# A new order of work in a fused attention and feed-forward kernel: later projection, moved weight sums, and a weight ring filled in three transfers a step

## The reference

```
xn  = layernorm(x)
att = layernorm(linear_attention(xn; 16 heads, elu+1) @ W_proj.T + b_proj) * gamma + beta + xn
h   = silu(xn @ w1.T * s1) * (xn @ w2.T * s2)          # 256 -> 1024
h   = gelu(h @ h1.T * sh1);  h = gelu(h @ h2.T * sh2)   # 1024 -> 1024, twice
out = x + att + (h @ w3.T) * s3                         # 1024 -> 256
```

## Time and profile before

| what | value |
|---|---|
| median of 3 runs | 1734.03 us (1733.47 to 1736.09) |
| profiled execution, whole | 1730.4 us |
| its span, first to last instruction | 1728.5 us |
| PE / PEld busy | 1562.2 us (90%) / 1438.9 us (83%) |
| DVE / ACT / POOL busy | 1213.1 us (70%) / 969.2 us (56%) / 501.1 us (29%) |
| moved by DMA | 298.15 MB |

### The profile page before, as it was taken

One profiled execution on the slowest core, in us unless ns is written; L12 is line 12 of the kernel. 1 busy time (PEld: TensorE's weight loads), 2 busy tenths in 40 slices (PEclk: granted clock), 3 DMA queues, 4 the chain that ended last, 5 costly groups with the idle time before them and its releaser, 6 DMA issues.

```text
span 1728.5 us, 32973 instructions
## 1 busy us (share of the span) xinstructions
PE 1562.2 (90%) x10956; PEld 1438.9 (83%) x10956; DVE 1213.1 (70%) x2083; ACT 969.2 (56%) x1745; POOL 501.1 (29%) x573
## 2 busy tenths in 40 slices
PE   6474999999999999999999999999999999999997
PEld 4474888888988888898888989888898888889897
DVE  3574686876868677685867768686685867768585
ACT  3243465655647465565755656565564656556463
POOL 3221150422314133240512314052231413323040
PEclk8697999999999999999999999999999999999999
DMA  6885255371735536173462626437172553717343
GB/s 229 316 325 187 92 205 182 109 255 51 263 106 182 195 112 234 57 252 138 140 232 91 228 89 227 162 116 254 52 260 98 195 186 113 243 43 261 129 159 132
DMA packets 84962, 298.15 MB, mean 172 GB/s; under 512 B 7232, under 2 KB 44224, under 8 KB 59584
## 3 DMA queue, kind: packets, MB, share of 16 engines
q0 software_dynamic: 37152, 238.04, 39.3%
q1 hardware_dynamic: 47344, 58.49, 10.0%
q10 hardware_dynamic: 432, 1.18, 0.2%
HBM read 280.91 MB, written 23.07 MB: 176 GB/s over the span
## 4 chain that ended last, share of the span: by engine, by line
PE 43%; DVE 20%; issue 16%; ACT 10%; DMA 4%; POOL 3%; DVEq 1%; SPq 0%; ACTq 0%; POOLq 0%
PE ps L830 19%; PE ps L859 7%; PE ps L804 5%; DVE partial_sums L1284 4%; PE ps L709 4%; DVE operands_a L1261 4%; PE ps L710 3%; PE ps L711 3%; DVE values_a L1253 3%; DVE operands_b L1261 2%; ACT operands_a L1008 2%; ACT values_out L1033 2%; ACT gate_ring L971 2%; POOL values_a L609 2%; DMA weight_set<-in_w_ffn 2%
## 5 line engine op out<-in xcount | busy, mean ns | idle before, releaser
L830 PE MATMUL ps<-operands_a,hidden_weights 128*128 128x256 f32 x5376 | 755.1, 286 | 61.6 <-DVE operands_a L1261 36.7
L830 PEld LDWEIGHTS ps<-operands_a,hidden_weights 128*128 128x128 f32 x5376 | 686.4, 191 | 88.1 <-DVE operands_a L1261 49.4
L830 PE MATMUL ps<-operands_b,hidden_weights 128*128 128x256 f32 x1792 | 298.2, 288 | 56.9 <-DVE partial_sums L1284 42.1
L830 PEld LDWEIGHTS ps<-operands_b,hidden_weights 128*128 128x128 f32 x1792 | 247.3, 191 | 69.6 <-DVE partial_sums L1284 45.8
L1284 DVE TENSOR_TENSOR partial_sums<-partial_sums,ps 128x512 f32<-128x512 f32 x320 | 214.3, 681 | 126.1 <-PE ps L830 125.5
L1261 DVE TENSOR_TENSOR operands_a<-values_a,operands_a 128x512 fp32r<-128x512 f32 x336 | 272.2, 825 | 41.9 <-ACT operands_a L996 22.3
L625 POOL DMA_DIRECT2D hidden_weights<-weight_blocks x252 | 138.0, 548 | 523.4 <-PE ps L830 510.6
L804 PE MATMUL ps<-xnT,w_ffn 128*128 128x512 f32 x1024 | 252.2, 401 | 15.3 <-DVE values_a L1253 15.3
L804 PEld LDWEIGHTS ps<-xnT,w_ffn 128*128 128x128 f32 x1024 | 191.7, 190 | 59.9 <-DVE values_a L1253 16.2
L1033 ACT ACTIVATE values_out<-partial_sums,vectors 128x256 f32<-128x256 f32 x192 | 86.9, 500 | 181.1 <-DVE partial_sums L1284 179.6
L1008 ACT ACTIVATE operands_a<-values_a 128x512 fp32r<-128x512 f32 x192 | 120.9, 630 | 107.8 <-POOL values_a L619 49.3
(11 more groups left out here) (112 smaller groups left out, 2083.2 us busy)
## 6 DMA issues: line engine op xcount, KB each, us to landing
hidden_weights<-weight_blocks POOLq DMA_DIRECT2D x192, 1024.0 KB, 5.6
hidden_weights<-weight_blocks POOLq DMA_DIRECT2D x64, 512.0 KB, 3.8
raw_weights<-weight_blocks SPq DMA_DIRECT2D x48, 272.0 KB, 5.5
x<-in_H SPq DMA_DIRECT2D x16, 512.0 KB, 5.1
weight_set<-in_w_ffn SPq DMA_DIRECT2D x16, 512.0 KB, 10.7
out_dram<-acc SPq DMA_DIRECT2D x32, 256.0 KB, 2.2
weight_blocks<-in_w_ffn SPq DMA_DIRECT2D x12, 512.0 KB, 10.6
weight_blocks<-weight_set SPq DMA_DIRECT2D x4, 1536.0 KB, 7.2
```

Of the source, the lines that this page charges most:

```text
L830: r = mm(bank[:, m * HT:(m + 1) * HT], ring_weights[:, place, 2 * g + j, m * P:(m + 1) * P], as_used(buf[:, j, slot[block_of_b], part, :]) ...
```

## The change: what it does

1. **Matmul order in a product.** The loop over the two halves m of the output goes inside the loops over group and part. All four matmuls of one group's hi (or lo) follow each other, so that the second group's hi is first needed at half the product and its lo at three quarters, where it was a quarter and three eighths.
2. **Ring parts.** Three transfers a step: block 1; blocks 5, 6, 7; blocks 2, 4, 3 (512, 1536, 1536 KB), each begun when the last product that uses it is through.
3. **Banks.** Even steps use banks 4, 5, 0 and odd ones 1, 2, 3; step 0's first product waits for the sixth gate group's value in place of the seventh's.
4. **Order on PE.** `kv_sums(1)` goes behind gate group 5, gate group 2 ahead of `apply_kv`; both `proj_step`s go from before step 1 to behind its second product. In tile 0 the transposes for tile 1 go from step 2 to step 3.
5. **Order on DVE, ACT and POOL.** `ln2_apply` (three passes over 128x1024) goes from the middle of step 3 to the end of the tile, behind the last `lo_of_output`; the last `output` goes behind all of the k, v work. `keep_first`, `add_u` and the second sum get waits for the GELU of the step before, which reads the same scratch. `keep_first(0)` is ahead of four conversions; `k_act_step` waits for `q_made`.
6. **Weight sets.** POOL's `weight_sums` is gone: DVE makes the sums of set 0 in the prologue, of set 1 in step 0, of set 2 in step 1 and of set 3 in step 2. SP loads set 2 after set 1 is stored and set 3 after step 1's last product; x of tile 1 is requested ahead of the store of set 3. SP no longer waits for `proj_weights` first, and DVE no longer for the warm-up.

Of the diff, the parts that the steps rest on:

```diff
-RING_PARTS = ((0, 1), (1, 2), (3, 2), (5, 2))
-PART_OF = {1: 0, 5: 1, 6: 1, 7: 2, 2: 2, 4: 3, 3: 3}
+RING_PARTS = ((0, 1), (1, 3), (4, 3))
+PART_OF = {1: 0, 5: 1, 6: 1, 7: 1, 2: 2, 4: 2, 3: 2}
-BANKS = ((0, 1, 4), (5, 2, 3), (0, 1, 4), (5, 2, 3))
-PART_FREE = ((1, 6, 2, 3), (1, 5, 7, 4), (1, 6, 7, 3), (1, 5, 7, 4))
+BANKS = ((4, 5, 0), (1, 2, 3), (4, 5, 0), (1, 2, 3))
+PART_FREE = ((1, 7, 3), (1, 7, 4), (1, 7, 3), (1, 7, 4))
...
-        return {(0, 1): gated(6), (0, 6): gated(6), (0, 5): gated(5),
+        return {(0, 1): gated(5), (0, 6): gated(5), (0, 5): gated(6),
...
@@ SP, tile 0
                         store_sums(1)
                         sp.wait_ge(s_stored[1], 32)
+                        load_set(2)
+                        copy_blocks(2)
+                        store_sums(2)
+                        sp.wait_ge(*prod.after(t, "1P4"))
                         load_set(3)
                         copy_blocks(3)
+                        load_x(t + 1, first)
                         store_sums(3)
-                        sp.wait_ge(s_stored[3], 32)
-                        load_x(t + 1, first)
@@ SP, prologue
-                sp.wait_ge(s_proj_raw, 16)
                 load_set(0)
                 copy_blocks(0)
-                sp.wait_ge(s_wproj, 2)
-                load_set(2)
                 store_sums(0)
-                copy_blocks(1)
-                store_sums(2)
                 sp.wait_ge(s_stored[0], 32)
                 load_set(1)
-                copy_blocks(2)
+                copy_blocks(1)
@@ PE, product
-                    for m in range(2):
-                        for g, group in enumerate(groups):
-                            buf, slot = operands(group)
-                            for part in range(2):
+                    for g, group in enumerate(groups):
+                        buf, slot = operands(group)
+                        for part in range(2):
...
+                            for m in range(2):
                                 for j in range(2):
@@ PE, body
                     product(t, 0, 3)
+
+                    product(t, 1, 1)
+                    product(t, 1, 6)
                     proj_step(t, 0)
                     proj_step(t, 1)
-
-                    product(t, 1, 1)
-                    product(t, 1, 6)
@@ ACT
             def keep_first(t, s):
                 act.wait_ge(*prod.after(t, f"{s}P1"))
+                if s > 0:
+                    act.wait_ge(*gelu.after(t, f"{s - 1}C21" if s % 2 else f"{s - 1}C12"))
@@ DVE
             def add_u(t, s):
                 dve.wait_ge(first_kept.sem, first_kept.at(t, s))
+                if s > 0:
+                    dve.wait_ge(*gelu.after(t, f"{s - 1}C12" if s % 2 else f"{s - 1}C21"))
                 sum_into(t, s, 6, 1, 0)
@@ DVE, prologue
-                    if checking:
-                        dve.wait_ge(s_warm, WARM_UP)
...
+                        sum_of_weights(0, 1)
+                        sum_of_weights(0, 3)
```

More of the change, by code:

```diff
@@ L680, in body @@
                             refill(t, 3, 2)
-                            refill(t, 3, 3)
                 return body
@@ L880, in body @@
                 def body(t, more):
+                    staging = isinstance(t, int) and t == 0
                     gate_group(t, 0)
@@ L920, in body @@
                     product(t, 2, 7)
-                    if more:
+                    if more and not staging:
                         transposes(t + 1, 0)
@@ L928, in body @@
                     product(t, 3, 6)
+                    if staging:
+                        transposes(t + 1, 0)
+                        transposes(t + 1, 1)
                     product(t, 3, 2)
@@ L1505, in body @@
                         check_piece(t, 0)
+                    if checking:
                         check_piece(t, 1)
-                        check_piece(t, 2)
-                    if checking:
-                        check_piece(t, 3)
-                    add_u(t, 3)
-                    lo_of_output(t, 0, "C12")
-                    add_v(t, 3)
+                    if more:
+                        transposed_lo(t + 1, 1)
+                    add_v(t, 3)
+                    lo_of_output(t, 0, "C22")
@@ new lines, in body @@
+                    add_c22(t, 3)
+                    lo_of_output(t, 0, "C21")
+                    lo_of_output(t, 0, "C12")
+                    add_c12(t, 3)
+                    add_c21(t, 3)
+                    lo_of_output(t, 1, "C22")
+                    lo_of_output(t, 1, "C12")
+                    if checking:
+                        check_piece(t, 2)
+                    if more:
+                        put_ones(t + 1)
+                    lo_of_output(t, 0, "C11")
+                    lo_of_output(t, 1, "C21")
@@ L1537, in body @@
-                    output(t, 1)
-                    if more:
                         z_step(t + 1, 2)
                         z_step(t + 1, 3)
+                        phi_k(t + 1, 0)
+                        if checking:
+                            check_piece(t, 3)
+                        phi_k(t + 1, 1)
                         phi_k(t + 1, 2)
                         phi_k(t + 1, 3)
+                    else:
+                        if checking:
+                            check_piece(t, 3)
+                            dve.wait_ge(piece_checked.sem, piece_checked.at(t, CHECKS - 1))
+                            v.tensor_reduce(low_max[:], low[:], AX_X, ALU.max).then_inc(s_low_step, 1)
+                        output(t, 0)
+                        if checking:
+                            dve.wait_ge(s_flag_sum, 1)
+                            v.tensor_copy(flag[:], att_bank(A_T0)[0:1, 0:1]).then_inc(s_flag, 1)
@@ L1544, in run @@
+                    output(t, 1)
                 over_tiles(dve, first, prologue, body)
```

299 lines of the change are left out of this document (145 added, 154 removed).

## The result

The changed kernel takes 1791.58 us (median of 4 runs, 1785.17 to 1793.6), the kernel before 1733.75 us beside it (1732.32 to 1736.09): ratio 1.0326, 95% interval 1.0297 to 1.0354. I had said 1646 us, and 1603 to 1692 as the range. The profiled execution of the changed kernel has this head, where the one before has 1728.5.

A forecast was written before the change was run, and what follows sets the result against it. PE was taken as the bound, its waits as what could be won. Tile 1 beginning at 169, 14 loop tiles of 97.9 and a last tile of 101.7 gave 1641.3 us span, predicted as 1646 us, range 1603 to 1692.

The forecast's parts named there:

- The stops for operands and sums: Product stretch of a loop tile: 8.5 us of PE stops go, one operand wait of 0.6 us stays.
- a floor of 93.6 us without the ring: Loop tile: 102.14 less 0.6 in the gate phase and 8.5 in products, plus 0.6 for one wait.
- `ln2_apply` at its later place: End of the loop tile: its move there costs PE 0, with 1 us of cover.
- The ring in three transfers: Loop tile: larger refills land after the products that need them, costing 4.3 us a tile.
- the 2.8 us for blocks 2, 4, 3 of step 3: Free after step 2's last product, needed two products or 3.8 us later, so late 2.8 us.
- The landing of 6.5 us: Time for 1536 KB to land in the ring, 6.6 us with POOL's wake of 0.1; bounds 5.1 and 9.6.
- Tile 0: First tile: tile 1 begins near 169 us in place of 197.2, 28 us earlier; bounds 42 and 10.
- The end: Last tile: more work ahead of the reduction adds 5.2 us; the last tile takes 101.7 us.
- The sum: Whole kernel: 169 + 14 x 97.9 + 101.7 = 1641.3 us span, 1643 profiled execution, 1646 predicted.
- The rivals: Alternative outcomes for the whole kernel: 1613 us (chance 0.17), 1684 (0.16), 1709 (0.06), 1871 (0.05), 1734 (0.02).
- The slower one: Loop tile: 1536 KB refills land in 12 us or more, 15 us a tile, 1871 us; chance 0.05.
- my three signs of being wrong: 1536 KB landings over 8 us, DVE releasing PE for over 2 us a tile, or tile 1 beginning after 187.

The follow-up runs named there:

- e1_four: Changed kernel with the ring filled in four smaller transfers a step in place of three: 1598.20 us, ratio 0.9198 to 0.9229.
- e5_small_x: Changed kernel with the load of the next tile's x cut from 512 KB to 64 KB: 1758.18 us, ratio 1.0126 to 1.0184.
- e8: Changed kernel with four ring transfers a step, plus raw weight block copies of sets 2 and 3 begun one set earlier: 1588.71 us.
- e6_block_waits: Changed kernel with the same three releases a step, but each block moved and waited for alone: 1669.47 us, ratio 0.9618 to 0.9653.
- e9: Changed kernel with added matmuls, results unused, before all six waits for the ring from tile 1 on: 1759.45 us, ratio 1.0134 to 1.0173.

## Why the prediction was wrong, point by point

- **The stops for operands and sums: right.** I took 8.5 us of stops off the products, left 0.6, and had a floor of 93.6 us without the ring. e1_four measures 93.44, and the one stop left in the tile read is 0.38 us, for an operand. `ln2_apply` at its later place costs PE nothing: no stop stands in the end of e1_four's tile.
- **The ring in three transfers: the step that failed.** The term was 4.3 us a tile; it measures 12.8. The mechanism was the one named, a part that lands behind the product that needs it; the size was off by three. By pair of steps I had 0.3, 1.2 and 2.8 us of stops; the trace has 3.08 (step 0 to 1), 3.40 (1 to 2) and 3.25 (2 to 3). So the 2.8 us for blocks 2, 4, 3 of step 3 was right (2.86), and the four stops of steps 1 and 2 measure 6.5 us where I had 1.5. Three things were missing. The landing of 6.5 us holds only for a transfer that runs alone: the chain has 9.19 us (issued at 757.63, behind the part beside which x is loaded) and 8.53 (777.24, behind the part issued at 773.47). POOL's issue begins 0.5 to 0.6 us after the product ends at the three refills of the chain, not 0.1, for which no row stood. And the clock, for which I had nothing, takes 2.2. Stops and clock make 11.9 of the 12.8 us; the last 0.9 I can't assign, and idle times are modelled.
- **What I read past.** The earlier trace rows had 9.6 us for two blocks amid traffic. I wrote it down as the upper bound of the landing and never worked out the stops that it gives. The estimate from the Trainium skill (DMA: Bandwidth & Descriptors, on the fixed cost of a transfer), 5.6 us for 1536 KB, would have made the error larger: the 1536 KB loads into the ring have medians from 6.5 us (e5_small_x) up.
- **Tile 0: 28 us forecast, 9 found, below my lower bound of 10.** The first gate and product came 5 us late (33.88 and 52.49 for 29 and 47.6), step 1 ended at 107.86 instead of 96, and blocks 5, 6, 7 of set 3 landed at 152.58 instead of 133. I had priced loads, sums and stores, and not the copies of raw blocks nor the wait of POOL for them. e8 shows 11 us of it, on the order with four transfers. Part of the other 8 stands in the chain, and I had it at nothing: I counted tile 0's products at full clock, and the granted clock from 52.49 to 188.15 is 0.82. Sixteen matmuls in the chain take there what thirty-two take at full clock:

```profile
82.84 3.76 PE ps L828 x16
...
90.46 3.80 PE ps L828 x32
...
104.05 3.79 PE ps L828 x16
...
152.72 3.75 PE ps L828 x16
```

  That is 1.9 us more at each of the three, 5.6 in all. No run takes it away, so how much earlier tile 1 would begin is not shown.
- **The end.** The last tile measures 1790.1 - 1675.59 = 114.5 against 101.7; without the ring's waits it is 102.7 (e1_four), so that term was right. (My 101.3 for the last tile before rested on one tile of 102.14; with the mean of 102.34 it is 98.6, and the forecast did not use it.)
- **The sum.** 14 x (106.25 - 97.9) = 117, tile 0 19, last tile 13: 149 us, all of the gap between 1643 and the profiled 1791.9.
- **The rivals.** The slower one was to decide from 10.3 us of ring waits a tile. That point was right, and the ring's 12.8 us passed it, with the clock; the stops alone, 9.7, fall just short of it. Its condition, a landing of 12 us or more, did not come: 9.19 is the longest in the chain of the loop tile. Its price (15 us on top) was too high and its chance, 0.05, too low. I had argued against it from the DMA share of the whole tile, 0.48, but the refills that matter run in bursts: the share is 1.03 in the window 799 to 801.
- **The signs.** One of my three signs of being wrong came, tile 1 after 187 us (188.15). The rows of 1536 KB read 7.4 us, not over 8, and DVE releases PE for 0.38 us a tile. None of the three watched the sum of the ring's stops, where the loss lay.

## What to carry to other kernels

When stops of one kind are taken out of a pipelined loop, the transfers lose what cover those stops gave (the same three cost 8.2 us a tile on the old order and 12.8 on the new): work out each refill's slack in the new, shorter schedule, with the landing time of that size beside its own neighbours, not alone. Fewer, larger transfers into a ring make the first block wait for the last; cut parts by when each block is freed and needed. The issues that they save cost PE nothing here at four a step (e1_four), but at seven a step POOL's issues stood in the chain (e6_block_waits). A stop of PE of some 2 us or more cost in many tiles another 1.7 us of full-clock work behind it, so price a stop with its clock.

## What the runs showed of the hardware that I had not expected

- The granted clock fell to 0.50 behind stops of 2.05 us (start to start, at 570.64) as well as of 3.14 us, and not behind every stop of that length (784 to 786, 2.01 us, has none). In windows of 1 us each fall takes 1.7 us of full-clock work or, in some tiles, 3.4; over tiles 1 to 14 of the changed kernel they sum to 41 us, 2.9 a tile, where e9 recovers 2.2.
- Seven transfers of 512 KB a step, issued in groups, land in 5.6 us in the median (e6_block_waits), single ones in 3.9 (e1_four): a small transfer is late when others were issued just before it.
- What stays open: 0.9 us a tile of the ring's 12.8, and what tile 0 would gain at full clock.
